# First layer of a four-layer graph network: four row biases added on VectorE instead of by products, hs scaled on ScalarE, a ring of 10 word tiles

## The reference

```python
Wh = h @ W
e = leaky_relu(Wh @ a_src + (Wh @ a_dst).T, 0.2)
attn = softmax(where(adj > 0, e, -9e15), axis=1)
h_attn = attn @ Wh
h_enh = silu(_ln(Wh @ fe1_w + fe1_b, fe_ln_g, fe_ln_b)) @ fe2_w + fe2_b
B, C, dt = split(Wh @ W_bcdt + b_bcdt, 3, axis=1)
ab = softmax(dt + A[None, :], axis=1) * B @ abp_w + abp_b
h_part, z = split((Wh * ab) @ W_hz + b_hz, 2, axis=1)
hs = (h_part * silu(z) + h_part * D) @ out_w + out_b
hs = hs * (1.0 + C @ cp_w + cp_b)
g = sigmoid(silu(_ln(concat([h_attn, hs]) @ g1_w + g1_b, g_ln_g, g_ln_b)) @ g2_w + g2_b)
out = _ln(g * h_attn + (1.0 - g) * hs + h_enh, ln_g, ln_b)
```

## Time and profile before

| | us |
|---|---|
| median of 3 executions | 2262.12 (2261.96 to 2262.26) |
| the profiled execution | 2261.55 |
| its span, first to last instruction | 2259.9 |
| PE busy | 2193.8 |
| DVE busy | 1500.1 |
| ACT busy | 1083.2 |
| POOL busy | 114.8 |
| mean granted clock of TensorE | 0.992 of full speed |

### The profile page before, as it was taken

How to read it: one execution, slowest core, us unless ns; L and a number is a source line. 1 busy time by engine, 2 the same in 40 slices (tenths; PEclk the granted TensorE clock), 3 DMA queues, 4 the chain that set the end, 5 groups by cost and what they waited for, 6 DMA issues and landing times. The chain is left out here.

```text
span 2259.9 us, 43206 instructions
## 1 busy us (share of the span) xinstructions
PE 2193.8 (97%) x17096; PEld 1688.8 (75%) x17096; DVE 1500.1 (66%) x2311; ACT 1083.2 (48%) x1592; POOL 114.8 (5%) x123
## 2 busy tenths in 40 slices
PE   5899999999999998999979999999999999999999
PEld 4777777777777777888868888887466666666667
DVE  6855657575665745222256656665898898898897
ACT  6444353444435356666662111213465565665556
POOL 2000001010100101000000000000000000000000
PEclk9999999999999999999989999999999999999999
DMA  7643141424411112222312222222111111111010
GB/s 185 126 64 52 50 85 43 85 42 80 62 57 47 46 63 77 90 88 88 102 43 66 82 72 79 70 82 86 52 33 48 33 52 48 34 52 47 24 33 29
DMA packets 63404, 146.77 MB, mean 65 GB/s; under 512 B 10087, under 2 KB 15354, under 8 KB 62237
## 3 DMA queue, kind: packets, MB, share of 16 engines
q1 hardware_dynamic: 57037, 111.09, 15.8%
q0 software_dynamic: 5664, 33.16, 9.0%
q10 hardware_dynamic: 560, 0.52, 0.1%
HBM read 170.43 MB, written 41.43 MB: 94 GB/s over the span
## 5 line engine op out<-in xcount | busy, mean ns | idle before, releaser
L198 PE MATMUL bank<-s_row,kT_hi 128*128 128x512 f16 x1024 | 305.7, 380 | 3.8 <-DVE m_col L2797 1.2
L2186 PE MATMUL bank<-VB,arena 128*128 128x257 f16 x1024 | 280.9, 274 | 2.9 <-issue 2.9
L2189 PE MATMUL bank<-VB,arena 128*128 128x257 f16 x1024 | 280.1, 274 | 0.0
L2187 PE MATMUL bank<-VB,arena 128*128 128x257 f16 x1024 | 280.0, 273 | 0.0
L2914 PE MATMUL bank<-VA,w_dense 128*128 128x257 f16 x1008 | 276.2, 274 | 3.4 <-ACT w_dense L2735 2.4
L2916 PE MATMUL bank<-VA,arena 128*128 128x257 f16 x1008 | 275.9, 274 | 0.0
L2915 PE MATMUL bank<-VA,w_dense 128*128 128x257 f16 x1008 | 275.8, 274 | 0.0
L2186 PE MATMUL bank<-VB,ph 128*128 128x257 f16 x912 | 204.1, 274 | 7.9 <-ACT ph L2044 5.0
L2187 PE MATMUL bank<-VB,ph 128*128 128x257 f16 x912 | 204.0, 274 | 0.0
L198 PE MATMUL bank<-s_row,kT_lo 128*128 128x512 f16 x512 | 194.8, 380 | 0.0
L1590 PE MATMUL bank<-VA,p_words 128*128 128x257 f16 x688 | 188.5, 274 | 1.5 <-DVE p_words L1190 1.5
(11 more groups left out here) (355 smaller groups left out, 4832.7 us busy)
## 6 DMA issues: line engine op xcount, KB each, us to landing
quad_ring<-mask_d SPq DMA_DIRECT2D x185, 256.0 KB, 2.7
mask<-mask_d SPq DMA_DIRECT2D x71, 256.0 KB, 2.9
mask_d<-in_adj POOLq DMA_DIRECT2D x8, 2048.0 KB, 23.5
xg<-in_x SPq DMA_DIRECT2D x8, 512.0 KB, 13.1
x<-xg SPq DMA_DIRECT2D x8, 512.0 KB, 3.9
xg<-x SPq DMA_DIRECT2D x8, 512.0 KB, 4.2
x<-xo POOLq DMA_DIRECT2D x8, 512.0 KB, 3.0
w_dense<-x SPq DMA_DIRECT2D x8, 512.0 KB, 4.3
```

The costliest lines, as they stand in the source:

```text
L198: last = nc.tensor.matmul(out_ap, st, mv, start=(i == 0), stop=(i == len(todo) - 1))
L2186: nc.tensor.matmul(acc, p_hi, v_at(V, 0, t), start=first, stop=False)
L2187: last = nc.tensor.matmul(acc, p_hi, v_at(V, 1, t), start=False, stop=final and not weighted)
L2189: last = nc.tensor.matmul(acc, p_lo, v_at(V, 0, t), start=False, stop=final)
```

## The change

Four of the six row biases leave the products (bcdt, fe2, out, g2; fe1 and g1 stay). They are loaded as rows spread over the 128 partitions, `row_b` in fp32, and DVE adds them: bcdt in place in PSUM, out while it takes hs from PSUM to SBUF, fe2 while it moves the rows to `wr` (ACT did), g2 while it moves the rows to `TH`, from where ACT now takes tanh. hs is scaled by ACT, in SBUF. `turn_c(f, 0)` moves behind tile 3. The ring has 10 tiles, 6 and 4, and the fp16 masks of the next layer lie in the first four of it. A row of W1's bias that nothing read is dropped. `tops`, a later layer's buffer, moves from `bias3` to `row_b`.

```diff
-    for name, n in [("bcdt", 2 * S), ("fe1", H), ("fe2", D), ("out", D), ("g1", H), ("g2", D), ("W1", D)]:
+    for name, n in [("fe1", H), ("g1", H)]:
-        bias3 = sb(top, "bias3", [P, bias_n + bias_n % 2], F16)
+        row_b = sb(top, "row_biases", [P, 4, D], F32)
+        bias3 = sb(front, "bias3", [P, bias_n], F16)
-        col_loads = 11
+        col_loads = 14
...
+                                            (row_b[:, BFE, :], "L0_gnn_fe2_b"), (row_b[:, BOUT, :], "L0_gnn_out_b"),
+                                            (row_b[:, BG2, :], "L0_gnn_g2_b"))]
...
+                    load(sp, row_b[:, BDT, 0:S], a["L0_gnn_b_bcdt"][0:S].partition_broadcast(P), s_bias)
+                    load(sp, row_b[:, BDT, S:2 * S], a["L0_gnn_b_bcdt"][2 * S:3 * S].partition_broadcast(P), s_bias)
+                    load(sp, arow, a["L0_gnn_A"].partition_broadcast(P), s_bias)
...
-                        nc.vector.tensor_tensor(brow[:, :], brow[:, :], arow[:, :], ALU.add).then_inc(bias_cut.sem, 1)
+                        nc.vector.tensor_tensor(row_b[:, BDT, S:2 * S], row_b[:, BDT, S:2 * S], arow, ALU.add
+                                                ).then_inc(summed_c.sem, 1)
...
-            PR = 12
-            PO = 8
+            PR = 10
+            PO = 6
...
-                ph = pw[:, PO // 2:PO, :].rearrange("p t n -> p (t n)").bitcast(F16).rearrange("p (t n) -> p t n", t=HR)
+                ph = pw[:, 0:HR // 2, :].rearrange("p t n -> p (t n)").bitcast(F16).rearrange("p (t n) -> p t n", t=HR)
...
-                    def keep_fe2(d, j):
-                        act.wait_ge(fe2_made.sem, fe2_made.upto(2 * d + j))
-                        if d:
-                            act.wait_ge(s_wst, 16 * d)
-                        b = (AB + 1, CD + 1)[j]
-                        nc.scalar.copy(half(wr, j), bank[b][:, :]).then_inc(fe2_kept.sem, 1)
+                    def scale_hs(d):
+                        act.wait_ge(out_added.sem, out_added.upto(d))
+                        for r in range(R):
+                            last = nc.scalar.mul(row(hsr, r), row(hsr, r), c1[:, d * R + r:d * R + r + 1])
+                        last.then_inc(hs_made.sem, 1)
...
                     def gate_tanh(f, j):
-                        act.wait_ge(g2_made.sem, g2_made.upto(2 * f + j))
-                        act.wait_ge(sT_lo.sem, sT_lo.upto(2 * f + j))
-                        b = (AB, CD)[j]
-                        nc.scalar.activation(half(TH, j), bank[b][:, :], ACT.Tanh, scale=0.5).then_inc(tanhed.sem, 1)
+                        act.wait_ge(g2_added.sem, g2_added.upto(2 * f + j))
+                        nc.scalar.activation(half(TH, j), half(TH, j), ACT.Tanh, scale=0.5).then_inc(tanhed.sem, 1)
...
-                            if hq == 1 and i >= 1:
-                                keep_fe2(d - 1, 1)
                             if hq == 2 and i >= 1:
                                 scale_rows(f)
+                                scale_hs(d - 1)
                             if hq == 2:
                                 keep_whT(d)
...
                             if hq == 13:
                                 if i >= 1:
                                     gate_tanh(f, 0)
-                                keep_fe2(d, 0)
...
                     gate_tanh(G - 2, 1)
-                    keep_fe2(G - 1, 1)
                     scale_rows(G - 1)
+                    scale_hs(G - 1)
                     next_masks(0, 4)
...
+                    def add_row(dst, src, which, n):
+                        return nc.vector.tensor_tensor(
+                            dst.rearrange("p (r n) -> p r n", n=D), src,
+                            row_b[:, which:which + 1, :].broadcast_to([P, n, D]), ALU.add)
...
                     def take_hs(d):
...
-                        for r in range(R):
-                            last = nc.vector.tensor_scalar(row(hsr, r), cell(AB, r), c1[:, d * R + r:d * R + r + 1], None,
-                                                           ALU.mult)
-                        last.then_inc(hs_made.sem, 1)
+                        add_row(hsr[:, :], cells(AB), BOUT, R).then_inc(out_added.sem, 1)
+
+                    def add_fe2(d, j):
+                        dve.wait_ge(fe2_made.sem, fe2_made.upto(2 * d + j))
+                        if d:
+                            dve.wait_ge(s_wst, 16 * d)
+                        add_row(half(wr, j), two_cells((AB + 1, CD + 1)[j]), BFE, 2).then_inc(fe2_kept.sem, 1)
+
+                    def add_g2(f, j):
+                        dve.wait_ge(g2_made.sem, g2_made.upto(2 * f + j))
+                        dve.wait_ge(sT_lo.sem, sT_lo.upto(2 * f + j))
+                        add_row(half(TH, j), two_cells((AB, CD)[j]), BG2, 2).then_inc(g2_added.sem, 1)
...
+                    def add_bdt(d):
+                        dve.wait_ge(bdt_made.sem, bdt_made.upto(d))
+                        nc.vector.tensor_tensor(cells(CD), cells(CD), row_b[:, BDT:BDT + 1, :].broadcast_to([P, R, D]),
+                                                ALU.add).then_inc(bdt_added.sem, 1)
...
                                 mT_low(d - 1, 3)
+                                if i >= 2:
+                                    add_g2(z, 1)
+                                add_fe2(d - 1, 1)
...
                             if hq == 5:
+                                add_bdt(d)
                                 dt_max(d)
...
                             if hq == 13:
                                 fe_variance(d, 1)
                                 feT_low(d, 0)
+                                if i >= 1:
+                                    add_g2(f, 0)
+                                add_fe2(d, 0)
...
                     mT_low(G - 1, 3)
+                    add_g2(G - 2, 1)
+                    add_fe2(G - 1, 1)
...
                     last_sT_low(1)
+                    last_add_g2(0)
                     gate_u(G - 1, 0)
                     V_low(G - 2)
+                    last_add_g2(1)
                     gate_u(G - 1, 1)
...
-                            last = products(pe, cell(AB, r), [(cols(mT, m, r), w("out", m)) for m in range(HK)], "out")
+                            last = products(pe, cell(AB, r), [(cols(mT, m, r), w("out", m)) for m in range(HK)])
...
-                            if t == 2 and f >= 0:
+                            if t == 3 and f >= 0:
                                 turn_c(f, 0)
```

More of the change, by code:

```diff
@@ L180, in build @@
         BZ, BH, BABP, FEG, FEB, GG, GB = 0, 4, 8, 10, 14, 18, 22
+        BDT, BFE, BOUT, BG2 = range(4)
         def w(name, k, c0=0, c1=None):
@@ L337, in rows @@
                     return t[r0:r0 + n, :]
[L339 to L342, removed]
+                bias_rows = []
+                arow = junk[:, 8, S:2 * S]
+                for name, vec in (("fe1", "L0_gnn_fe1_b"), ("g1", "L0_gnn_g1_b")):
                     at, n = bias_at[name]
@@ L351, in opening @@
                 column_in = [(t[:, :], a[vec].partition_broadcast(P))
-                             for t, vec in ((Dcol, "L0_gnn_D"), (lng, "L0_gnn_ln_g"), (lnb, "L0_gnn_ln_b"))]
+                             for t, vec in ((Dcol, "L0_gnn_D"), (lng, "L0_gnn_ln_g"), (lnb, "L0_gnn_ln_b"),
+                                            (row_b[:, BFE, :], "L0_gnn_fe2_b"), (row_b[:, BOUT, :], "L0_gnn_out_b"),
+                                            (row_b[:, BG2, :], "L0_gnn_g2_b"))]
                 for at, vec in ((BH, a["L0_gnn_b_hz"][0:H]), (BZ, a["L0_gnn_b_hz"][H:2 * H]),
@@ L688, in first_layer @@
                     "hz_made", "hp_made", "z_made", "hz_multiplied", "mT_hi", "mT_lo")
-                (out_made, hs_made, fe2_made, fe2_kept, w_made) = counts(
-                    "out_made", "hs_made", "fe2_made", "fe2_kept", "w_made")
+                (out_made, out_added, hs_made, fe2_made, fe2_kept, w_made) = counts(
+                    "out_made", "out_bias_added", "hs_made", "fe2_made", "fe2_kept", "w_made")
+                (bdt_added, g2_added) = counts("bdt_bias_added", "g2_bias_added")
                 (cT_made, cT_hi, cT_lo, dl_made, g1_made) = counts("cT_made", "cT_hi", "cT_lo", "dl_made", "g1_made")
@@ L1061, in last_gate_tanh @@
                     def last_gate_tanh(j):
[L1062 to L1065, removed]
+                        act.wait_ge(g2_added.sem, g2_added.upto(2 * (G - 1) + j))
+                        nc.scalar.activation(half(TH, j), half(TH, j), ACT.Tanh, scale=0.5).then_inc(tanhed.sem, 1)
                     act.wait_ge(s_col, 16 * col_loads)
@@ L1292, in fuse, with cells, two_cells @@
                                                        ).then_inc(f_made.sem, 1)
+                    def add_row(dst, src, which, n):
+                        return nc.vector.tensor_tensor(
+                            dst.rearrange("p (r n) -> p r n", n=D), src,
+                            row_b[:, which:which + 1, :].broadcast_to([P, n, D]), ALU.add)
```

(29 more changed lines are left out.)

23 lines of the change are left out of this document (10 added, 13 removed).

## The result

| | before | after |
|---|---|---|
| median of 19 executions each, us | 2262.66 (2261.08 to 2264.07) | 2266.25 (2264.10 to 2267.83) |
| ratio, 95% interval | | 1.0015 (1.0009 to 1.0021) |
| profiled execution, us | 2261.55 | 2266.73 |
| its span, us | 2259.9 | 2265.0 |
| PE busy, us | 2193.8 | 2183.8 |

The changed kernel takes 3.6 us more, 0.16%, with an interval of 0.09% to 0.21%: more than nothing, but inside the 4.5 us that the prediction called no change.

The account below looks back on a forecast made before the run. PE, busy 97% of the span, was taken as the bound. Terms -4.2 + 0.9 + 5.7 = +2.4 us, with clock falls +1.5 and +1.2 making +5.1, on 2262.12 gave 2267.2 us; range 2262.8 to 2271.5.

Parts of the forecast that it names:

- rival 1: Same stalls, but the clock holds in one place or both: +2.4 to +3.9 us, 2264.5 to 2266.0; 40%.
- The products: First layer on PE: 128 bias products of 256 columns removed, 0.11 us each, 14.1 us, all on the path.
- The steady groups: Groups 1 to 7: late shift_of stalls turn_fe 1.16 us, so each keeps 0.60 of 1.76; -4.2 us in all.
- Group 0: First group: later turn_fe, less the removed biases, +0.9 us; a clock fall after 3.1 us of PE idle, +1.5.
- The layer's end: Masks behind scale_hs: PE idle 3.7 us, last_cT_low(1) late, +3.6 us; up to 1.2 more if the clock falls.
- g2 at the end: Last g2 adds on DVE delay tanh and V_low, so the last gate_u comes later: +2.1 us.
- the turn of c: Every group: moving turn_c(f,0) from tile 2 to tile 3 leaves project_bdt where it was; nothing lost.
- the add of bdt: DVE's PSUM add ahead of dt_max, 1.14 us each group, covered by ACT's wait of 3.2 us; no cost.
- The opening: Kernel start: three more loads on SP's queue and an equally long cut of biases on DVE; costs nothing.
- rival 2: Faster: no wait at turn_fe because DVE reaches shift_of earlier; -8.4 us, 2253.7; 6%.
- rival 3: Clock swings: half speed after each 1.16 us stall in seven groups, 10 us more, 2277; 5%.
- rival 4: The ring of 10 binds, or scale_hs delays keep_whT beyond its 1.9 us: 8 x 0.5, 2271; 2%.

Follow-up runs that it names:

- experiment 1: Changed kernel with shift_of for fe1's second half moved ahead of add_g2, add_fe2 and two weighings on DVE; median 2253.63 us, ratio 0.9959.
- experiment 3: Kernel before with the 128 products of the four row biases left out and nothing in their place, so output lacks them; median 2247.54 us, ratio 0.9931.
- experiment 2: Changed kernel with all six masks and last_cT_high(0) ahead of scale_hs on ACT at the layer's end; median 2261.92 us, ratio 0.9997.
- experiment 4: Changed kernel with last_add_g2(1) ahead of V_low(G-2) on DVE at the layer's end; one execution, 2267.08 us.
- experiment 7: Changed kernel with turn_c(f, 0) back behind tile 2; one execution, 2267.95 us.
- experiment 8: Changed kernel executed once more with nothing else changed; 2267.43 us.
- experiment 6: Kernel before with only the ring of 10 weight tiles in place of 12; median 2263.36 us, ratio 1.0003.
- experiment 5: Changed kernel with three reorderings together: shift_of earlier, masks ahead of scale_hs, last_add_g2(1) ahead of V_low(G-2); median 2246.24 us, ratio 0.9930.

## Why the prediction was right or wrong

The median, 2266.25, is inside the range and 0.95 below the 2267.2. The stalls are those of the prediction; the clock is not. The forecast, given 47%, had two falls of the clock on top of what was there, and rival 1 (2264.5 to 2266.0, 40%) at most one. The difference of 3.6 us lies within rival 1's own, 2.4 to 3.9, and the median 0.25 above its range. But the clock did not hold in group 0, as rival 1 says: it fell behind the new idle time, and no longer behind the old one. Neither case has this. The forecast also said slower by more than 4.5 us with 52%; 3.6 us is within what it called no change.

**The products** (14.1 us): right for the groups. 1.74 to 1.75 us a group, experiments 1 and 3.

**The steady groups** (a stall of 1.16, kept 0.60 a group, -4.2): right in mechanism, each step of the chain found in its place; experiment 1 undid it. Short in size: the stall is 1.18, and the transposes behind it take 0.93 us to the next start instead of 0.87, so 1.75 - 1.18 - 0.06 = 0.51 is kept, measured 0.50; the last of the seven groups keeps 0.32, and the seven together -3.4.

**Group 0** (+0.9, and +1.5 by the clock): this is the step that failed. "I count a fall: +1.5" put a second fall beside the one that the group already had behind its idle time of 2.4 us. It moved instead. Group 0 in parts, in us:

| | before | after | experiment 2 | experiment 3 |
|---|---|---|---|---|
| first tile to the start behind the idle time of 2.4 | 47.88 | 48.06 | 47.86 | 48.19 |
| to the transposes of fey | 8.44 | 8.38 | 9.65 | 6.56 |
| their idle time, in the row above | 1.12 | 2.95 | 2.55 | 1.12 |
| to the first `project_out` | 23.37 | 24.79 | 23.15 | 23.15 |
| the clock fell behind | 2.4 | 2.95 | 2.4 | none |

Experiment 3 has none of the group's eight biases, like after, and full speed from the idle time of 2.4 us on. Against it the fall cost 24.79 - 23.15 = 1.64 us in after, and before, with two more biases, 8.44 - 6.56 - 0.22 = 1.66: the price of a fall was about right, but it was paid once in either kernel. The stall is 2.95 - 1.12 = 1.83, less 8 x 0.11 for the biases, so +0.95, as predicted. The other 0.6 of the measured +1.54 is the longer half speed at the group's start, which was in no term: the first row is 0.18 longer with 0.44 us less in it. Experiment 2 does not show the stall alone: its +0.97 on before holds 0.4 of the same kind, and where the fall stays in its old place the idle time is 2.55 and not the 3.1 that was counted for that case. What went wrong is that I priced a fall by the nearest row and never asked whether the new one would come on top of the old one or instead of it.

**The layer's end** (+3.6, clock +1.2): the idle time was 3.56 where 3.7 was predicted; the fall came, and the two together are +4.6 instead of +4.8. Experiment 2 gave back 3.7 of them with the fall, and so left +0.9. About 0.9 of the 4.6 is the clock: in after ACT's second copy for the gate (`last_cT_high(1)`) waits 0.87 for PE's turn of hs, which comes behind two tiles mostly at half speed, and that copy holds `last_cT_low(1)`. Here the fall is repeatable: all five profiles with this idle time (after, experiments 1, 4, 7, 8) have a clock of 0.57 to 0.60 behind it.

**g2 at the end** (+2.1): +2.0, of which experiment 4 gave back 1.3. The 0.7 that is left is what the first add with its hand-over takes ahead of the tanh; no run shows it alone.

**Edits costed at nothing**: the ring (experiment 6), the turn of c (experiment 7), the add of bdt and the adds in general (experiment 1 against 3: the same period). The opening, costed at nothing, was 0.6 longer in the profile of after; the experiments with the same opening (1, 2, 4, 5, 7 and 8) had their first tile at 61.70, 62.22, 63.05, 61.88, 63.62 and 62.98, and experiments 3 and 6, with that of before, at 63.11 and 62.75. It is scatter.

**The sum.** That the profiles lie 5.1 us apart and the forecast said +5.1 is no confirmation of each term: group 0 was 0.9 too high, the seven groups 0.8 too low, the end 0.3 too high, and opening and later layers, +0.6 and -0.3, were in no term. The medians say 3.6, and the executions of one kernel are spread by more than these errors. That the forecast lies within 1 us is in part luck.

**The rivals.** No stall at all (rival 2) fell with the eight waits. A swinging clock (rival 3) fell with the window of groups 1 to 7: a clock of 1.00 over 686 us with seven idle times of 1.02 us in it. The Trainium skill (TensorE: Matmul & The Clock Gate, A second HAM failure mode) tells of a kernel whose frequent short idle times made the clock oscillate; this trace does not show that. The ring (rival 4) fell with experiment 6. "Faster" needed the stall to be under 0.3 us. Experiment 1 meets that and is 9 us faster than before, although it keeps the two losses of the end.

## What to carry to other kernels

When work moves from a full engine to one with room, the room is not the question; the order is. Look at each wait that the moved work brings, and at what short, already ready instruction stands behind it on the same engine and on whom it is urgent: here 0.16 us of work behind a wait held PE eight times, and a whole list of masks behind another held it once. In the steady groups a product removed from PE was worth its full 0.11 us once one of the three orders was mended, and then the adds on DVE were free; mending the other two gave back most of what the end had lost. And when a stall is priced with a fall of the clock, ask whether the stretch has a fall already.

## What the runs showed of the hardware that was not expected

The same instructions with the same idle time of 2.4 us in group 0 were followed by the level of 1.2 GHz in five profiles (before, experiments 1, 2, 5 and 6, mean clock 0.61 to 0.67 behind it) and by 2.4 GHz in five (after, experiments 3, 4, 7 and 8); experiment 2 and after have the same code there. In four of these the next idle time, of 2.9 us, took the fall; in experiment 3 the next one was 1.1, and there was none. In no profile did two idle times inside group 0 have a fall each, and experiment 2's idle time of 2.55, which came when its half speed had just ended, had none. After and experiment 8, the same kernel, agree on the place.

One thing goes with the place in all ten: how long the half speed at the group's start lasts. In the first 7 us from the first tile PE issued 43 to 47 products (47, 47, 43, 46 and 44 in before and experiments 1, 2, 5 and 6) where the clock then fell behind the 2.4 us, and 39 to 41 (41, 40, 39, 39 and 39 in after and experiments 3, 4, 7 and 8) where it did not. So what the clock does some 40 us later goes with how the opening ended. That this is the cause is not shown; no run set it on purpose.

Between the first tile and the next layer's own block, idle times of 1.0 to 1.7 us were followed by no fall in any of the ten. Those of 3.6 us, and those of 5 to 7 us ahead of that block, always were.

The executions of a kernel are spread by some 3 us, and this goes with the mean clock, while the waits of after and experiment 8, two executions of one kernel, agree to 0.1 us. Of the 19 executions of after, 15 had a mean clock of 0.990 and took 2266.4 on average, three had 0.991 and took 2264.3, and one had 0.989 and took 2267.8. Of the 15 of before beside experiments 1 to 4, 13 had 0.992 and took 2262.5, two had 0.991 and took 2263.9. So some 2 us of any one execution go with the clock it was granted, and a profile of a single execution can't settle a difference of that size.
